# Half of the mask transposes of visits 6 to 21 moved from TensorE to VectorE in a masked graph attention kernel

## The chip, the cores and the metric

The kernel runs on one core of a Trainium2 chip. The metric is the device time of one execution in microseconds (us). An engine's name in the profile is PE for TensorE (matmuls; PEld is its weight load), DVE for VectorE, ACT for ScalarE, POOL for GpSimd and SP for SyncE, which here issues most of the loads.

## The reference, cut to what matters

```python
# x: (8192, 256) f32, adj: (8192, 8192) int32 of 0 and 1, a: (512, 1)
h = jnp.maximum(_layernorm(x, axis=-1), 0.0)
h1 = h @ a[:256];  h2 = h @ a[256:]
e = leaky_relu(h1 + h2.T, 0.01)
attention = jnp.where(adj > 0, e, -9e15)
attention = softmax(attention, axis=1)
out = x + attention @ h
```

The kernel uses that exp(leaky_relu(h1 + h2)) is, up to factors of row and column, a maximum of two terms. For a pair (i, j) it computes a weight W = max(r_i, g_j) times the mask bit, and sums W times (q_j h_j) over j. The row's own factor falls out in the division by the sum of weights.

## The kernel before, in words

**Tiles.** The 8192 rows and 8192 columns of adj are cut in blocks of 512. A *chunk* is one block of rows against one block of columns: 1 MB of int32, 256 chunks in all. A *visit* works one block of rows against 4 chunks (visits 0 to 24, 26, 28, ...) or 8 chunks (the odd visits from 25 on). `n` counts pairs of chunks; the chunk in a pair is `kc`, 0 (even) or 1 (odd), and a visit of 4 chunks has two values of n. A chunk has two *steps*, each of two tiles of 128 columns, so n has four steps k = 0 to 3, and `g` = 4n + k counts steps.

**One chunk goes through five engines.**

1. SP loads it to `adj_in[:, kc]` (`load_adj`), as soon as ACT has converted the chunk that stood there before, two chunks earlier. In visits 0 to 21 that is one DMA of 1 MB in rows of 2 KB (L271). From visit 22 on it is four DMAs of 256 KB whose pieces are 512 B long and lie turned in blocks of 32 (L268).
2. ACT makes a mask of 1-byte numbers, `mask8[:, kc]` (`convert`, L542).
3. The mask must stand with columns on the partitions. In visits 0 to 21 TensorE transposes it, four 128x128 tiles a chunk, into the PSUM tile `T[:, kc]` (L917). From visit 22 on (`N_MID` = 44 is the first n of that part, `dt` = `LATE` = 4) VectorE does it, with one transpose of 32x32 blocks (L767) over data loaded turned.
4. For each step DVE computes the weights (`weights`, L786, two instructions of 512 columns, from `T[:, kc]`), ACT rounds them to `w_hi` (`round_w`, L555 or L552), and DVE subtracts, which gives the rest `w_lo` (`subtract`, L801 or L797).
5. TensorE multiplies and sums into `acc`, 24 matmuls a step (`products`, L950, L952, L953), 48 a chunk.

**The order on each engine is written out by hand.** DVE's step k of n is: subtract of the step two before (g - 2), then side work if any, then the weights of g. `weights` waits until that subtraction is finished (`s_lo`), since it writes the buffer `W[:, k % 2]` that the subtraction read. `subtract` waits for ACT (`s_hi`), and for TensorE to have used the `w_lo` buffer of two steps before (`s_used`). TensorE in n does the products of step 0, transposes the even chunk of n + 1, does steps 1 and 2, transposes the odd chunk of n + 1, does step 3. ACT's order is convert of chunk (n, 1), rounding of steps 0 and 1, convert of chunk (n + 1, 0), rounding of steps 2 and 3, with side work after a rounding.

**Side work.** Visits 1 to 4 each prepare four further row tiles of h ("whole"). From visit 5 to 20 a pair of visits does it: visits 5, 7, ..., 19 ("early") the statistics (L728, four, then four aggregates L734), visits 6, 8, ..., 20 ("late") the scores (L754, eight instructions, two in each of steps 4 to 7 of the visit). ACT has the rows of h (L479, two at each of the last two steps of an early visit), exponentials (L493 to L497) at the end of a late one, and rounds h (L513) at the start of the next early one. At the start of each visit ACT empties `acc` to `stage` (L574), POOL adds the earlier partial sums from visit 9 on (L410), and a store and a load of 516 KB go to and from HBM.

Of the kernel before, what the change touches and what calls it, by code (L numbers as in the profile page):

```python
# [9 lines left out]
def masked_graph_attention(nc, x, adj, a, out):  # L10
# [35 lines left out]
    MID, LATE = 0, 4  # L46
    N_MID = 2 * 22

# [12 lines left out]
    with ctx:  # L61
# [126 lines left out]
        def run(eng, steps, h_made=None, h_summed=None):  # L188
# [13 lines left out]
            def quarter(v, q, prev, make=None, phase=None, made=None, nxt=None, head=False, turn=False,  # L202
                        dt=MID, dt_next=MID, deep=False):
# [16 lines left out]
            def two(j, q1, q2, prev1, prev2, nxt=None, dt=MID):  # L220
# [27 lines left out]
        def _(sp):  # L248
# [41 lines left out]
            def steps(V, n, c, first, second, last, third=False):  # L290
                if V.head and first:
                    load_x(0, 0, False)
                    sp.dma_start(r_rep[:, 1, :], a_row.partition_broadcast(P)).then_inc(s_a, 16)
                for kc in range(CI):
                    if V.head and not first:
                        load_x(c + kc, kc, True)
                    if V.head and first and kc == 1:
                        load_x(1, 1, False)
                        sp.dma_start(x_ahead, x_w[2]).then_inc(s_xa, 16)
                    load_adj(V.b, c + kc, n, kc, not (V.head and first), V.dt)  # L300
# [157 lines left out]
        def _(act):  # L458
# [72 lines left out]
            def convert(n, kc, wait, dt):  # L531

                if dt < G:
                    act.wait_ge(s_adj[kc], 16 * (n + 1))
                if dt:
                    act.wait_ge(s_turn[kc], 64 * (n - N_MID + 1))
                if dt == G and not (isinstance(n, int) and n == N_MID):
                    act.wait_ge(s_TV, (n - N_MID) * CI + kc - 1)
                elif wait:
                    act.wait_ge(s_T, n * CI + kc - 1)  # L540
# [72 lines left out]
            def begin():  # L613
# [5 lines left out]
                convert(0, 0, False, 0)  # L619
# [6 lines left out]
            def head_chunk(m):  # L626
# [7 lines left out]
                convert((m + 1) // CI, (m + 1) % CI, m > 0, 0)  # L634
# [80 lines left out]
        def _(dve):  # L715
# [53 lines left out]
            def weights(V, c, c_tot, g, k, wait, enter=False):

                if V.dt < G:
                    dve.wait_ge(s_T, c_tot + 1)
                if V.dt:
                    dve.wait_ge(s_TV, c_tot - CI * N_MID + 1)
# [78 lines left out]
            def steps(V, n, c, first, second, last, third=False):  # L853
# [3 lines left out]
                for k in range(PI):  # L857
                    kc = k // 2
                    g = n * PI + k
                    if V.head:  # L860
                        m = c + kc if V.head else None
                        dve.wait_ge(s_ex, m + 1)
                        weights(V, m, n * CI + kc, g, k, not (first and k < 2))
# [5 lines left out]
                    else:  # L869
                        if V.dt and k % 2 == 0:  # L870
# [7 lines left out]
                        weights(V, c + kc, n * CI + kc, g, k, True, enter)  # L878
# [26 lines left out]
        def _(pe):  # L905
# [78 lines left out]
            def steps(V, n, c, first, second, last, third=False):  # L984
# [6 lines left out]
                for k in range(PI):  # L991
# [15 lines left out]
                    if k % 2 == 0 and not V.head and not (V.tail and last):  # L1007
                        transpose_mask(n + 1, kc, True, V.dt_next if last else V.dt)
# [28 lines left out]
```

## Time and profile before

| | |
|---|---|
| time, 3 runs | median 1552.14 us (1547.85 to 1553.05) |
| the profiled execution | 1552.08 us, of which its span is 1550.3 us |
| PE busy | 1522.7 us, 98% of the span |
| PEld busy | 1511.9 us, 98% |
| DVE busy | 1489.6 us, 96% |
| ACT busy | 1162.5 us, 75% |
| POOL busy | 457.4 us, 30% |
| DMA | 331.05 MB, mean 214 GB/s |
| granted TensorE clock | 0.999 |

The span is from the first to the last instruction of the profiled execution; its own time is 1.8 us longer. Busy times of different engines lie beside each other. PE's busy time is no measure of how full it is, since matmuls overlap; how fast chunks follow one another is. Visits 6 to 21 lie between about 180 and 574 us of the span, and the seven pairs of visits 7 to 20 between about 205 and 549 us.

### The profile page before, as it was taken

To read this page: it belongs to the slowest core of one execution; us is meant where nothing else is said; L and a number is where in the kernel's file an instruction comes from. 1 tells how busy PE (TensorE), PEld (TensorE's weight loads), DVE (VectorE), ACT (ScalarE), POOL (GpSimd) and SP (SyncE) were. 2 spreads that over 40 slices of the span, in tenths; PEclk is the share of its full clock that TensorE was granted. 3 is DMA by queue.
4 is the path that set the end of the run, shared out by engine and by line. 5 is a ranking of instruction groups with operands and counts; after the bars stand their busy time and mean duration, and the time that the engine had idled before them with its cause. 6 is when DMAs were issued, how large, how long until landed. Compare 5 with 4: busy or idle time off the path is not lost.

```text
span 1550.3 us, 38852 instructions
## 1 busy us (share of the span) xinstructions
PE 1522.7 (98%) x12678; PEld 1511.9 (98%) x12678; DVE 1489.6 (96%) x2172; ACT 1162.5 (75%) x1180; POOL 457.4 (30%) x547
## 2 busy tenths in 40 slices
PE   5999999999999999999999999999999999999999
PEld 5999999999999999999999999999999999999998
DVE  7999999999999999999999999999999999999998
ACT  7787877778777777677776876777777777677774
POOL 6363334335452340120420320320320320420420
PEclk9999999999999999999999999999999999999999
DMA  6666677787778799999999999999999999999994
GB/s 211 222 200 230 206 223 227 230 248 221 245 220 254 220 225 233 221 201 206 218 207 207 224 204 207 226 197 210 230 195 205 228 195 207 217 195 209 219 199 98
DMA packets 436493, 331.05 MB, mean 214 GB/s; under 512 B 16704, under 2 KB 378176, under 8 KB 436416
## 3 DMA queue, kind: packets, MB, share of 16 engines
q1 hardware_dynamic: 411360, 288.94, 83.6%
q10 hardware_dynamic: 25056, 41.13, 8.7%
q8 instruction: 43, 0.70, 0.2%
q14 instruction: 34, 0.28, 0.1%
HBM read 308.90 MB, written 21.10 MB: 213 GB/s over the span
## 4 chain that ended last, share of the span: by engine, by line
PE 82%; DMA 5%; DVE 3%; ACT 3%; issue 2%; SPq 1%; ACTq 0%; DVEq 0%
PE acc L950 27%; PE acc L953 26%; PE acc L952 26%; DMA adj_in<-in_adj_dram 5%; PE T L917 2%; ACT mask L542 2%; DVE w_lo L797 1%; DVE halves L786 1%; SPq L268 1%; ACT w_hi L552 0%; DVE T L767 0%; DVE w_lo L801 0%; ACT w_hi L555 0%; DVE adj_in L901 0%; DVE adj_in L896 0%
## 5 line engine op out<-in xcount | busy, mean ns | idle before, releaser
L950 PE MATMUL acc<-h_hi,w_hi 128*128 128x258 f32 (+1 forms) x4096 | 1167.3, 285 | 9.2 <-DVE w_lo L801 3.4
L953 PE MATMUL acc<-h_hi,w_lo 128*128 128x258 f32 (+1 forms) x4096 | 1153.3, 282 | 0.0
L952 PE MATMUL acc<-h_lo,w_hi 128*128 128x256 f32 (+1 forms) x4096 | 1149.7, 281 | 0.0
L950 PEld LDWEIGHTS acc<-h_hi,w_hi 128*128 128x128 f32 x4096 | 771.8, 188 | 17.8 <-issue 8.0
L952 PEld LDWEIGHTS acc<-h_lo,w_hi 128*128 128x128 f32 x4096 | 778.4, 190 | 0.1
L953 PEld LDWEIGHTS acc<-h_hi,w_lo 128*128 128x128 f32 x4096 | 775.3, 189 | 0.0
L786 DVE SCALAR_TENSOR_TENSOR halves<-r_rep,g_all,T 128x512 f32<-128x512 f32 (+1 forms) x1024 | 712.7, 736 | 10.8 <-PE T L917 1.5
L542 ACT ACTIVATE mask<-adj_in,mhalf 128x2048 fp8e5<-128x2048 int32 x256 | 510.3, 1993 | 58.8 <-DMA adj_in<-in_adj_dram 58.5
L552 ACT ACTIVATE w_hi<-halves 128x1024 fp32r<-128x1024 f32 x336 | 353.6, 1057 | 185.0 <-DVE halves L786 172.3
L797 DVE SCALAR_TENSOR_TENSOR w_lo<-halves,w_hi 128x1024 fp32r<-128x1024 f32 x336 | 418.2, 1245 | 9.9 <-PE acc L953 4.9
L555 ACT ACTIVATE w_hi<-halves 128x1024 fp32r<-128x1024 f32 x176 | 185.3, 1057 | 97.5 <-DVE halves L786 92.6
L801 DVE SCALAR_TENSOR_TENSOR w_lo<-halves,w_hi 128x1024 fp32r<-128x1024 f32 x176 | 230.7, 1311 | 17.7 <-PE acc L953 9.1
L419 POOL TENSOR_TENSOR xb<-xb,stage 128x256 f32<-128x256 f32 x60 | 49.9, 831 | 584.7 <-ACT stage L606 584.3
L410 POOL TENSOR_TENSOR stage<-stage,xo 128x258 f32<-128x258 f32 x96 | 94.1, 1014 | 196.1 <-ACT stage L574 139.5
L767 DVE STREAM_TRANSPOSE T<-mask 128x512 f32<-128x512 f32 x168 | 120.6, 718 | 6.7 <-ACT mask L542 6.7
L382 POOL TENSOR_SCALAR halves<-halves,q 128x256 f32<-128x256 f32 x56 | 37.6, 690 | 201.5 <-ACT q L497 172.8
L574 ACT ACTIVATE stage<-acc 128x258 f32<-128x258 f32 x156 | 56.3, 383 | 25.4 <-PE acc L953 24.4
L426 POOL TENSOR_TENSOR xb<-xb,halves 128x256 f32<-128x256 f32 x60 | 69.0, 1151 | 9.1 <-POOL halves L423 7.4
L917 PE MATMUL T<-ident,mask 128*128 128x128 f32 x352 | 53.5, 274 | 14.6 <-ACT mask L542 14.6
L423 POOL TENSOR_SCALAR halves<-halves,fin 128x256 f32<-128x256 f32 x60 | 56.2, 937 | 0.0
L917 PEld LDWEIGHTS T<-ident,mask 128*128 128x128 f32 x352 | 41.1, 141 | 15.5 <-issue 12.5
L390 POOL TENSOR_TENSOR hsum<-hsum,halves 128x256 f32<-128x256 f32 x48 | 50.6, 1054 | 2.8
(70 smaller groups left out, 343.8 us busy)
## 6 DMA issues: line engine op xcount, KB each, us to landing
adj_in<-in_adj_dram SPq DMA_DIRECT2D x672, 256.0 KB, 5.0
adj_in<-in_adj_dram SPq DMA_DIRECT2D x88, 1024.0 KB, 6.3
part_sums<-stage ACTq DMA_DIRECT2D x24, 516.0 KB, 5.6
xo<-part_sums ACTq DMA_DIRECT2D x24, 516.0 KB, 4.4
r_rep<-r_rows SPq DMA_DIRECT2D x39, 256.0 KB, 4.8
xb<-in_x_dram ACTq DMA_DIRECT2D x15, 512.0 KB, 5.9
out_dram<-xb ACTq DMA_DIRECT2D x15, 512.0 KB, 4.7
xb<-in_x_dram SPq DMA_DIRECT2D x14, 512.0 KB, 5.8
```

The costliest lines, as they stand in the source:

```text
L410: last = nc.gpsimd.tensor_tensor(stage[:, t, :], stage[:, t, :], prior[:, t, :], ALU.add)
L542: nc.scalar.activation(mask8[:, kc, :, :].rearrange("p t j -> p (t j)"), adj_in[:, kc, :, :].rearrange("p t j -> p (t j)"), ACT.Sign, bias ...
L552: nc.scalar.activation(w_hi[:, k % HL, :].rearrange("p (u j) -> p u j", u=2), deep_w[k], ACT.Relu).then_inc(s_hi, 1)
L555: nc.scalar.activation(w_hi[:, k % HL, :], W[:, k % 2, :], ACT.Relu).then_inc(s_hi, 1)
L767: nc.vector.transpose(T[:, kc, t * P:], mask_words[:, kc, t:G, :]).then_inc(s_TV, 1)
L786: last = nc.vector.scalar_tensor_tensor(out, r_rep[:, V.v % 2, :], g_all[:, ds(G * c + e, 1)], T8[:, k // 2, e, :], ALU.max, ALU.mult)
L797: nc.vector.scalar_tensor_tensor(w_lo[:, k % LL, :].rearrange("p (u j) -> p u j", u=2), deep_w[k], 0.0, w_hi[:, k % HL, :].bitcast(f32).re ...
L801: nc.vector.scalar_tensor_tensor(w_lo[:, k % LL, :], W[:, k % 2, :], 0.0, w_hi[:, k % HL, :].bitcast(f32), ALU.max, ALU.subtract).then_inc ...
L917: last = nc.tensor.transpose(T[:, kc, t * P:(t + 1) * P], mask_words[:, kc, t, :], ident[:])
L950: nc.tensor.matmul(acc[:, t, 0:WC], w_hi[:, k % HL, cols], rhs_hi, start=start and u == 0, stop=False)
L952: nc.tensor.matmul(acc[:, t, 0:D], w_hi[:, k % HL, cols], rhs_lo, start=False, stop=False)
L953: last = nc.tensor.matmul(acc[:, t, 0:WC], w_lo[:, k % LL, cols], rhs_hi, start=False, stop=stop and u == 1)
```

## The change

In visits 6 to 21 (n = 12 to 43, 64 chunks) the even chunk of each n is handled as before: a plain load, four transposes by TensorE. The odd chunk is now loaded turned, with four DMAs, and transposed by one VectorE instruction. `dt` becomes a pair, one entry for each kc: `PLAIN` (0, 0), `ALT` (0, 4), `LATE` (4, 4). Visits 0 to 5 and 22 on stay as they were.

```diff
-    MID, LATE = 0, 4
+    PLAIN, ALT, LATE = (0, 0), (0, 4), (4, 4)
+    N_ALT = 2 * 6
     N_MID = 2 * 22
+    FIRST_TURNED = (N_MID, N_ALT)
+    def count_turned_by_tensor(n, kc, form):
+        return n * CI + kc + 1 if form == PLAIN else n + N_ALT + 1
+    def count_turned_by_vector(n, kc, form):
+        return n - N_ALT + 1 if form == ALT else N_MID - N_ALT + (n - N_MID) * CI + kc + 1
...
                 for q in range(4 if dt else 0):
-                    sp.dma_start(adj_in[32 * q:32 * q + 32, kc, G - dt:G, :],
-                                 adj_turned[b, :, 4 * (G - dt):4 * G, ds(c * BLK + q * P, P)]).then_inc(s_turn[kc], 16)
-                if dt < G:
-                    sp.dma_start(adj_in[:, kc, 0:G - dt, :], adj_v[b, :, 0:G - dt, ds(c * BLK, BLK)]
-                                 ).then_inc(s_adj[kc], 16)
+                    sp.dma_start(adj_in[32 * q:32 * q + 32, kc, :, :],
+                                 adj_turned[b, :, :, ds(c * BLK + q * P, P)]).then_inc(s_turn[kc], 16)
+                if not dt:
+                    sp.dma_start(adj_in[:, kc, :, :], adj_v[b, :, :, ds(c * BLK, BLK)]).then_inc(s_adj[kc], 16)
...
             def transpose_mask(V, n, kc):
-                if V.dt < G:
-                    dve.wait_ge(s_T, g + 1)
-                else:
-                    dve.wait_ge(s_mask, g + 1)
+                dve.wait_ge(s_mask, n * CI + kc + 1)
                 dve.sem_inc(s_vgate, 1)
-                nc.vector.transpose(T[:, kc, t * P:], mask_words[:, kc, t:G, :]).then_inc(s_TV, 1)
+                nc.vector.transpose(T[:, kc, :], mask_words[:, kc, :, :]).then_inc(s_TV, 1)
...
-                        if V.dt and k % 2 == 0:
+                        if V.dt == LATE and k % 2 == 0:
                             transpose_mask(V, n, kc)
...
-                        weights(V, c + kc, n * CI + kc, g, k, True, enter)
+                        if V.dt == ALT and k == 1:
+                            transpose_mask(V, n, 1)
+                        weights(V, c + kc, n, g, k, True, enter)
...
-                        transpose_mask(n + 1, kc, True, V.dt_next if last else V.dt)
+                        transpose_mask(n + 1, kc, True, (V.dt_next if last else V.dt)[kc])
```

`convert` waits in the same way as before, for the load and for whoever transposed the chunk that stood in `mask8[:, kc]`; `weights` waits for VectorE's count of transposes (`s_TV`) for an odd chunk of visits 6 to 21 and for TensorE's (`s_T`) for an even one.

On VectorE, at the start of visit 7, these rows stood before (L801 is a subtraction, L728 a statistic, L786 the two weights):

```order
L801 SCALAR_TENSOR_TENSOR w_lo<-halves,w_hi 128x1024
L786 SCALAR_TENSOR_TENSOR halves<-r_rep,g_all,T 128x512 x2
L801 SCALAR_TENSOR_TENSOR w_lo<-halves,w_hi 128x1024
L728 BN_STATS bst<-xb 128x6
L786 SCALAR_TENSOR_TENSOR halves<-r_rep,g_all,T 128x512 x2
L801 SCALAR_TENSOR_TENSOR w_lo<-halves,w_hi 128x1024
L728 BN_STATS bst<-xb 128x6
```

With the change the same place reads (L810 is the subtraction, L742 the statistic, L795 the weights, L776 the new transpose):

```order
L810 SCALAR_TENSOR_TENSOR w_lo<-halves,w_hi 128x1024
L795 SCALAR_TENSOR_TENSOR halves<-r_rep,g_all,T 128x512 x2
L810 SCALAR_TENSOR_TENSOR w_lo<-halves,w_hi 128x1024
L742 BN_STATS bst<-xb 128x6
L776 STREAM_TRANSPOSE T<-mask 128x512
L795 SCALAR_TENSOR_TENSOR halves<-r_rep,g_all,T 128x512 x2
L810 SCALAR_TENSOR_TENSOR w_lo<-halves,w_hi 128x1024
L742 BN_STATS bst<-xb 128x6
```

The transpose of chunk (n, 1) stands in step 1 of n, behind the side work and ahead of the weights of the even chunk, which do not need it. It needs ACT's convert of chunk (n, 1).

On SP, over visit 7 and the start of visit 8, these rows stood before (L271 is the plain load of a chunk, L261 the load of rows of x, L287 that of `r_rep`):

```order
L261 DMA xb<-in_x_dram 128x1024
L271 DMA adj_in<-in_adj_dram 128x4x512 x2
L287 DMA r_rep<-r_rows 128x512
L271 DMA adj_in<-in_adj_dram 128x4x512 x4
```

With the change there stands (L280 is the plain load, L277 the turned one, L270 the load of x, L295 that of `r_rep`):

```order
L270 DMA xb<-in_x_dram 128x1024
L277 DMA adj_in<-in_adj_dram 32x16x128 x4
L280 DMA adj_in<-in_adj_dram 128x4x512
L295 DMA r_rep<-r_rows 128x512
L277 DMA adj_in<-in_adj_dram 32x16x128 x4
L280 DMA adj_in<-in_adj_dram 128x4x512
L277 DMA adj_in<-in_adj_dram 32x16x128 x4
L280 DMA adj_in<-in_adj_dram 128x4x512
```

Each odd chunk is now four issues in place of one; the number of bytes is the same.

## Rows read from the trace of the kernel before

**Rows 1.** Windows: us, busy of PE, PEld, DVE, ACT, POOL, clock, DMA share, GB/s

```profile
204.60:549.00 344.40, 344.40 (x2915) 344.40 (x2913) 324.59 (x504) 269.13 (x307) 140.11 (x168) 1.00 0.75 232
574.30:597.40 23.10, 23.10 (x195) 23.05 (x194) 22.91 (x29) 17.07 (x17) 3.02 (x4) 1.00 1.14 229
1104.80:1196.00 91.20, 91.20 (x768) 91.07 (x767) 90.34 (x117) 66.90 (x57) 15.16 (x16) 1.00 1.04 210
```

**Rows 2.** The chain that ended last: start us, us, what; visits 1 to 20

```profile
97.58 0.44 PE T L917 x4
...
149.12 0.44 PE T L917 x4
...
204.61 0.44 PE T L917 x4
...
549.01 0.44 PE T L917 x4
```

**Rows 3.** VectorE's groups from 204.6 to 549.0 us: busy, mean ns | idle before

```profile
L801 DVE SCALAR_TENSOR_TENSOR w_lo<-halves,w_hi 128x1024 fp32r<-128x1024 f32 x112 | 148.1, 1323 | 12.7 <-PE acc L953 7.7 <-ACT w_hi L555 4.7
```

**Rows 4.** Timeline of VectorE, end of visit 13, start of visit 14

```profile
369.41 1.41 DVE L786 SCALAR_TENSOR_TENSOR halves<-r_rep,g_all,T 128x512 f32<-128x512 f32 x2
370.73 1.22 DVE L801 SCALAR_TENSOR_TENSOR w_lo<-halves,w_hi 128x1024 fp32r<-128x1024 f32 x1
372.05 1.41 DVE L786 SCALAR_TENSOR_TENSOR halves<-r_rep,g_all,T 128x512 f32<-128x512 f32 x2
373.99 1.23 DVE L801 SCALAR_TENSOR_TENSOR w_lo<-halves,w_hi 128x1024 fp32r<-128x1024 f32 x1 [0.53 <-PE acc L953]
```

**Rows 5.** Timeline of VectorE, a statistic and the aggregates (visit 11)

```profile
303.85 1.21 DVE L801 SCALAR_TENSOR_TENSOR w_lo<-halves,w_hi 128x1024 fp32r<-128x1024 f32 x1
304.98 0.41 DVE L728 BATCH_NORM_STATS2 bst<-xb 128x6 f32<-128x256 f32 x1
305.32 1.38 DVE L786 SCALAR_TENSOR_TENSOR halves<-r_rep,g_all,T 128x512 f32<-128x512 f32 x2
...
309.70 1.24 DVE L801 SCALAR_TENSOR_TENSOR w_lo<-halves,w_hi 128x1024 fp32r<-128x1024 f32 x1 [0.22 <-ACT w_hi L555]
...
311.73 0.72 DVE L786 SCALAR_TENSOR_TENSOR halves<-r_rep,g_all,T 128x512 f32<-128x512 f32 x1
```

**Rows 6.** Timeline of VectorE, a step with two scores (visit 2)

```profile
89.99 1.22 DVE L801 SCALAR_TENSOR_TENSOR w_lo<-halves,w_hi 128x1024 fp32r<-128x1024 f32 x1
...
91.80 1.40 DVE L786 SCALAR_TENSOR_TENSOR halves<-r_rep,g_all,T 128x512 f32<-128x512 int8 x2
```

**Rows 7.** Timeline of VectorE, a transpose of the late stretch

```profile
1304.37 0.72 DVE L767 STREAM_TRANSPOSE T<-mask 128x512 f32<-128x512 f32 x1
1305.00 1.20 DVE L797 SCALAR_TENSOR_TENSOR w_lo<-halves,w_hi 128x1024 fp32r<-128x1024 f32 x1
```

**Rows 8.** Timeline of ScalarE beside rows 4

```profile
370.85 1.06 ACT L555 ACTIVATE w_hi<-halves 128x1024 fp32r<-128x1024 f32 x1 [0.52 <-DVE halves L786]
371.81 1.08 ACT L479 ACTIVATE halves<-xb,shift,rstd 128x256 f32<-128x256 f32 x2
372.80 1.99 ACT L542 ACTIVATE mask<-adj_in,mhalf 128x2048 fp8e5<-128x2048 int32 x1
```

**Rows 9.** Plain load, line L271, from 204.6 to 549.0 us

```profile
L271 SPq DMA_DIRECT2D adj_in<-in_adj_dram x56: 367/372/383, 210.3 to 547.9; - x56
...
DMA to landing us min/median/max: 5.1/6.3/9.4
```

**Rows 10.** Turned load, line L268, from 574 to 621 us (visits 22, 23)

```profile
L268 SPq DMA_DIRECT2D adj_in<-in_adj_dram x32: 311/489/1721, 578.4 to 620.8; - x32
...
DMA to landing us min/median/max: 4.1/5.7/9.1
```

**Rows 11.** Waits from 545 to 640 us: us in total, times, longest

```profile
ACT mask L542 <- DMA adj_in<-in_adj_dram: 14.6, 9, 3.4
...
DVE T L767 <- ACT mask L542: 1.6, 2, 0.8
```

More of the change, by code:

```diff
@@ L218, in finals, with two @@
                             head=False, tail=tail, dt=LATE, dt_next=LATE, deep=True, rest=None))
-            def two(j, q1, q2, prev1, prev2, nxt=None, dt=MID):
+            def two(j, q1, q2, prev1, prev2, nxt=None, dt=ALT):
                 quarter(5 + 2 * j, q1, prev1, make=SH + j, phase="early", made=SH - 1 + j, nxt=nxt, dt=dt)
                 quarter(6 + 2 * j, q2, prev2, make=SH + j, phase="late", turn=q2 != q1)
-            quarter(0, 0, None, head=True, dt=0, dt_next=0)
-            quarter(1, 0, "first", make=Q, phase="whole", dt=0, dt_next=0)
+            quarter(0, 0, None, head=True, dt=PLAIN, dt_next=PLAIN)
+            quarter(1, 0, "first", make=Q, phase="whole", dt=PLAIN, dt_next=PLAIN)
             with eng.Fori(2, 5) as v:
-                quarter(v, 0, "first", make=v + 3, phase="whole", made=v + 2, dt=0, dt_next=0)
-            two(0, 0, 0, "first", "first", dt=0)
+                quarter(v, 0, "first", make=v + 3, phase="whole", made=v + 2, dt=PLAIN, dt_next=PLAIN)
+            two(0, 0, 0, "first", "first", dt=PLAIN)
             two(1, 0, 1, "first", "first", nxt=0)
@@ L299, in steps @@
                         sp.dma_start(x_ahead, x_w[2]).then_inc(s_xa, 16)
-                    load_adj(V.b, c + kc, n, kc, not (V.head and first), V.dt)
+                    load_adj(V.b, c + kc, n, kc, not (V.head and first), V.dt[kc])
                     if V.phase in ("early", "whole") and first and kc == 0:
@@ L529, in early_round_h, with convert @@
                                          scale=q4[:, parity, e:e + 1]).then_inc(s_hh if e == G - 1 else s_h0, 1)
-            def convert(n, kc, wait, dt):
-                if dt < G:
+            def convert(n, kc, wait, form):
+                if form[kc]:
+                    act.wait_ge(s_turn[kc], 64 * (n - FIRST_TURNED[kc] + 1))
+                else:
                     act.wait_ge(s_adj[kc], 16 * (n + 1))
[L535 to L538, printed above, removed]
+                was = form
+                if isinstance(n, int) and n == N_ALT and form == ALT:
+                    was = PLAIN
+                if isinstance(n, int) and n == N_MID:
+                    was = ALT
+                if wait and was[kc]:
+                    act.wait_ge(s_TV, count_turned_by_vector(n - 1, kc, was))
                 elif wait:
-                    act.wait_ge(s_T, n * CI + kc - 1)
+                    act.wait_ge(s_T, count_turned_by_tensor(n - 1, kc, was))
                 act.sem_inc(s_gate, 1)
@@ L618, in begin @@
                 h_rows(0, 0, range(G))
-                convert(0, 0, False, 0)
+                convert(0, 0, False, PLAIN)
                 exps(0, 0)
@@ L633, in head_chunk @@
                     h_rows(m + 1, (m + 1) % CI, [2, 3])
-                convert((m + 1) // CI, (m + 1) % CI, m > 0, 0)
+                convert((m + 1) // CI, (m + 1) % CI, m > 0, PLAIN)
                 round_w(2 * m + 1, (2 * m + 1) % PI, 2 * m + 1 >= HL)
@@ L758, in transpose_mask, with weights @@
             def transpose_mask(V, n, kc):
-                g = n * CI + kc
-                t = G - V.dt
-                if V.dt < G:
-                    dve.wait_ge(s_T, g + 1)
-                else:
-                    dve.wait_ge(s_mask, g + 1)
-                dve.sem_inc(s_vgate, 1)
-                nc.vector.transpose(T[:, kc, t * P:], mask_words[:, kc, t:G, :]).then_inc(s_TV, 1)
[L769 to L774, printed above, removed]
+                dve.wait_ge(s_mask, n * CI + kc + 1)
+                dve.sem_inc(s_vgate, 1)
+                nc.vector.transpose(T[:, kc, :], mask_words[:, kc, :, :]).then_inc(s_TV, 1)
+            def weights(V, c, n, g, k, wait, enter=False):
+                if V.dt[k // 2]:
+                    dve.wait_ge(s_TV, count_turned_by_vector(n, k // 2, V.dt))
+                else:
+                    dve.wait_ge(s_T, count_turned_by_tensor(n, k // 2, V.dt))
                 if wait and (not V.deep or enter):
@@ L862, in steps @@
                         dve.wait_ge(s_ex, m + 1)
-                        weights(V, m, n * CI + kc, g, k, not (first and k < 2))
+                        weights(V, m, n, g, k, not (first and k < 2))
                         if m + 1 < Q:
```

2 lines of the change are left out of this document (1 added, 1 removed).

## The prediction

> **What bounds the kernel now.** The busy times come first: PE is busy 98% of the span and DVE 96%, so two engines are candidates, and a share of busy time can't say which of them sets the pace. The chain that ended last decides it. In visits 7 to 20 it stays on PE; the transposes of L917 lie in it, 0.44 us for each four, and they recur twice for each n, that is once for each chunk: from 204.61 to 549.01 us are 344.4 us, 56 chunks, 6.15 us each [rows 2]. The window of the same stretch shows PE and PEld busy for all of it at a granted clock of 1.00 [rows 1]. So PE sets the pace there. In the late stretch, where it transposes nothing, PE gets through 768 matmuls, 16 chunks, in 91.2 us, 5.70 us each [rows 1]; 6.15 less 0.44 is 5.71, so 0.44 us is what a chunk's transposes cost on PE, and nothing else differs.
>
> The next thing to read is how much room DVE has in those visits. Its group of subtractions shows 12.7 us of idle time ahead of it, 7.7 for PE and 4.7 for ACT [rows 3]. That is 3.7% of the stretch. The change takes 3.6% of PE's work in a pair of chunks away and gives DVE an instruction, so it has to be seen whether DVE can follow.
>
> **DVE's work, step by step, from start to start.** A bare step is 1.32 us from weights to subtraction and 1.32 us from subtraction to weights: 369.41, 370.73, 372.05 [rows 4], 2.64 in all. With a statistic between subtraction and weights, it is 303.85 to 305.32, 1.47 us in place of 1.32: 0.15 more. The statistic itself takes 0.34, but it starts 1.13 us behind the subtraction, 0.19 earlier than the weights could, which wait for the subtraction's end [rows 5]. The fourth statistic with its aggregates makes it 2.03 us, 0.71 more [rows 5]. Two scores make it 1.81, 0.49 more [rows 6]. A pair of visits (16 steps) thus wants 16 x 2.64 + 3 x 0.15 + 0.71 + 4 x 0.49 = 45.4 us, the seven pairs of visits 7 to 20 want 317.5 us. Subtractions that run beside POOL's work are longer: the mean is 1.323 us against 1.22 bare [rows 3, 4], 112 x 0.10 = 11.3 us. Sum 328.8 us, the low bound of DVE's need. The high bound comes from the other side: 344.4 less the 12.4 us waited for PE and ACT is 332.0 [rows 1, 3]. A recorded wait is a little short (0.53 stands beside a start 1.94 us behind the weights where 1.32 was possible, 0.62 lost [rows 4]), so I take 330, nearer to the low bound.
>
> **What the change removes.** 32 odd chunks no longer pass through PE: 32 x 0.44 = 14.1 us off PE. In visits 7 to 20 PE then wants 344.4 - 28 x 0.44 = 332.1 us.
>
> **What it adds on DVE.** The transpose took 0.63 us from its start to the next instruction's start [rows 7]. Put between a subtraction and weights, it fills the 0.19 us of waiting there: 1.13 + 0.63 - 1.32 = 0.44 us net. In step 1 of an early visit's first n a statistic has already filled that gap, in step 1 of a late visit's second n two scores have; there it costs 0.63. A pair of visits has two of each kind: 2.14 us, seven pairs 15.0 us. The Trainium skill ("VectorE: DVE Perf Modes", section "The DRAIN you can't avoid") says that each VectorE instruction drains before the next whatever is waited for, and that a semaphore between two costs nothing extra. The trace disagrees by the 0.19 us of rows 4 and 5; by the rule all 32 transposes cost 0.63 us, 20.2 us in place of my 16.9, and the forecast would be 3.3 us higher.
>
> **A wait it adds.** The transpose in step 1 of n waits for ACT's convert of chunk (n, 1), and everything behind it on DVE waits with it, though the weights of step 1 need only the even chunk. PE waits for those in turn. At the start of a late visit ACT rounds the last step of the visit before, makes two rows of h, then converts: 370.85, 371.81, 372.80 to 374.79 us [rows 8]. DVE, had it not waited 0.62 us for PE there, would have been at the transpose at 372.05 + 1.32 + 1.13 = 374.50 [rows 4, 5]. So the transpose is 0.29 us late, in 7 of these visits: 2.0 us, and once more in visit 6. At other n ACT has exponentials (shorter), or DVE has side work in step 0 of the second n; there the convert is done first, but at the start of an early visit by some 0.2 us only.
>
> **The sum.** DVE's need in visits 7 to 20: 330 + 15.0 + 2.0 = 347.0 us, with the bounds 345.8 and 349.0, against 344.4 now and 332.1 that PE wants. DVE becomes the engine that sets the pace, all along: PE's steps would be 5.93 us a chunk in the mean, and DVE's 6.2. The stretch gains nothing and loses 2.6 us (1.4 to 4.6). Visit 6 is a late visit: its transposes cost DVE 0.44 + 0.63 + 0.29, with much the same room as the others, so about nothing. Visit 21 has no side work on DVE: 8 x 2.64 + 2 x 0.44 + about 1 for POOL = 23.0 us, so PE's 0.44 us of the one odd transpose that it had there are gained: -0.4.
>
> **The loads.** SP issues four DMAs for an odd chunk in place of one: 0.49 us each in the median where there was 0.37 [rows 9, 10], so the last is out 1.5 us later. For each GB/s the turned loads keep the DMA engines busier: 1.04 at 210 GB/s against 0.75 at 232 [rows 1]. Half the chunks turned, I estimate 0.75 + 85 x (1.04/210 - 0.75/232) = 0.90, under the 1.04 at which the late visits lose nothing. The slowest plain load took 9.4 us, and the slowest turned piece 9.1 [rows 9, 10]; an odd buffer is free for two chunks less a convert, 12.3 - 2.0 = 10.3 us. Slowest piece plus issue, 10.6, is just too long; the median, 5.7 + 1.5, has room. I put 1 us for it. It is hidden by ACT's own work elsewhere. The whole is +2.6 - 0.4 + 1 = +3.2 us on the profiled 1552.08 us, which lies at the median (1552.14): **1555 us**.
>
> **Rivals.**
>
> *A: DVE follows, PE keeps the pace.* All 14.1 us come back, 1538 us. For it: PE is full all the time and DVE idle 3.7%. Against it: DVE's need must be below 332.1 - 17.0 = 315 us in visits 7 to 20, and its bare instructions alone are 317.5. Visits 1 to 4 speak against it too: each has the side work of a whole pair, and its chunks follow at (149.12 - 97.58) / 8 = 6.44 us, 25.8 us a visit [rows 2]. There DVE already sets the pace, and my prices give 8 x 2.64 + 3.1 = 24.2 and some 0.6 for POOL, so they are short there, not long. I give it 0.05. A part of it is more likely: my prices of DVE are 2% too high (the subtractions beside POOL fall otherwise, or 330 hides waits), then -7 us, 1545. 0.09.
>
> *B: the forecast*, DVE's need within -4 and +4 us of the above: 0.56, own range 1551 to 1560.
>
> *C: the masks of odd chunks are late (the slower side).* In visits 22 and 23, with all chunks turned and the same partial sums stored and loaded, ACT waited for loads 9 times, 14.6 us in all over some 16 chunks [rows 11], where in visits 7 to 20 the same view lists no such wait. There the transposes lost only 1.6 us, but they stand at the start of step 2; in the changed visits they stand at step 1, about 1.5 us sooner. It decides once an odd load is more than ACT's 0.2 us of room late. The 13 visits 9 to 21 have such traffic, two odd chunks each; 26 x (14.6 / 16) = 24 us of late converts at most, less the room at each second n, about half: +10 us behind B, 1565 us. Half of the bytes being plain speaks against it. 0.30. The Trainium skill ("DMA: Bandwidth & Descriptors", section "Specifications") puts the smallest transfer for line rate at 512 B, which is just what a turned piece has. By it the share would stay at 0.75 and this rival would hardly be possible; the shares of rows 1 say that such pieces do cost more, so I keep it.
>
> **How the numbers follow.** What this kernel's measurement can tell from no change is 0.3%, 4.7 us. Faster by more: A and nearly all of its part, 0.13. Slower by more, above 1556.8: C's 0.30 and the upper part of B, 0.12: 0.42. Within: 0.45. The range runs from 1547, below which only A and a part of the second case lie (0.10), to 1566, above which a tenth lies.
>
> **What would show it.** In the windows of visits 7 to 20, PE's gaps appear and DVE's idle ahead of the subtractions (now 12.7 us) falls to nearly nothing; chunks follow at 6.15 to 6.25 us. The transposes have 0.72 us each and are followed at 0.63. DVE's waits list the transpose behind ACT's convert, 8 times for about 0.3 us; many more, or over 1 us, with ACT waiting for loads, is C. The DMA share rises to 0.90. If instead the chunks follow at 5.9 us with PE full, it is A, and my sum of DVE's need was wrong. The stretches before 180 and behind 574 us keep their length.

## The result, and the profile after

The changed kernel took 1555.97 us in the median of 11 runs (1551.56 to 1559.69), the kernel before 1552.29 beside it (1547.85 to 1555.48). The ratio is 1.0023, with a 95% interval of 1.0012 to 1.0034: slower by 3.7 us, less than the 0.3% named in the prediction. The profiled execution was the slowest of the 11 (1559.69 us, span 1557.8 against 1550.3 before). Of these 7.5 us, 2.8 lie behind visit 21 and 1.2 ahead of visit 1, where the program is the same; so the stretches are compared one by one.

The windows of the changed kernel over the first and the third stretch of [rows 1], with the same columns:

```profile
204.60:549.00 344.40, 335.86 (x2774) 331.07 (x2773) 335.92 (x529) 263.38 (x304) 134.62 (x165) 1.00 0.90 229
...
1104.80:1196.00 91.20, 90.44 (x754) 89.65 (x753) 89.13 (x115) 66.87 (x57) 18.14 (x20) 1.00 1.04 206
```

PE is no longer busy all the time in visits 7 to 20: 335.9 of 344.4 us, and PEld 331.1, at the same granted clock. DVE went from 324.6 to 335.9. The DMA share rose from 0.75 to 0.90 at nearly the same GB/s.

VectorE's groups of the changed kernel in the same stretch, busy time and mean ns, then idle time before them and what ended it:

```profile
L810 DVE SCALAR_TENSOR_TENSOR w_lo<-halves,w_hi 128x1024 fp32r<-128x1024 f32 x111 | 147.3, 1327 | 0.0
...
L776 DVE STREAM_TRANSPOSE T<-mask 128x512 f32<-128x512 f32 x28 | 20.1, 717 | 2.5 <-ACT mask L556 2.4
```

The 12.7 us that DVE waited ahead of its subtractions [rows 3] are gone, and 2.4 us of waits for the mask are new. The waits of PE, DVE and ACT in that stretch (us in all, times, longest) say who waits now:

```profile
PE acc L961 <- ACT w_hi L569: 3.3, 7, 0.6
PE acc L961 <- ACT stage L588: 3.3, 7, 0.5
DVE T L776 <- ACT mask L556: 2.4, 7, 0.3
...
ACT mask L556 <- DMA adj_in<-in_adj_dram: 0.9, 2, 0.5
```

PE waits for rounded weights and for emptied sums. Both hang on DVE's pace: ScalarE empties the sums behind a rounding, and at 379.23 us that rounding had waited 1.32 us for DVE's weights. Loads are late for 0.9 us only. VectorE's timeline at the start of visit 14 is the place of [rows 4]:

```profile
372.91 1.22 DVE L810 SCALAR_TENSOR_TENSOR w_lo<-halves,w_hi 128x1024 fp32r<-128x1024 f32 x1
374.23 1.41 DVE L795 SCALAR_TENSOR_TENSOR halves<-r_rep,g_all,T 128x512 f32<-128x512 f32 x2
375.56 1.22 DVE L810 SCALAR_TENSOR_TENSOR w_lo<-halves,w_hi 128x1024 fp32r<-128x1024 f32 x1
377.12 0.73 DVE L776 STREAM_TRANSPOSE T<-mask 128x512 f32<-128x512 f32 x1 [0.35 <-ACT mask L556]
377.75 1.36 DVE L795 SCALAR_TENSOR_TENSOR halves<-r_rep,g_all,T 128x512 f32<-128x512 f32 x2
379.04 1.22 DVE L810 SCALAR_TENSOR_TENSOR w_lo<-halves,w_hi 128x1024 fp32r<-128x1024 f32 x1
380.36 1.41 DVE L795 SCALAR_TENSOR_TENSOR halves<-r_rep,g_all,T 128x512 f32<-128x512 f32 x2
381.68 1.76 DVE L810 SCALAR_TENSOR_TENSOR w_lo<-halves,w_hi 128x1024 fp32r<-128x1024 f32 x1
```

The subtraction at 375.56 follows the weights after 1.33 us, where it waited for PE before. The transpose then waits 0.35 us for the mask, and the next instruction follows 0.63 us behind it.

From here on the *stretch* is measured on VectorE, from the first weights of visit 7 to the first of visit 21. The two rows of the changed kernel are

```profile
201.75 1.41 DVE L795 SCALAR_TENSOR_TENSOR halves<-r_rep,g_all,T 128x512 f32<-128x512 f32 x2
...
549.60 1.41 DVE L795 SCALAR_TENSOR_TENSOR halves<-r_rep,g_all,T 128x512 f32<-128x512 f32 x2
```

so 347.8 us. In the kernel before they are

```profile
200.48 0.75 DVE L786 SCALAR_TENSOR_TENSOR halves<-r_rep,g_all,T 128x512 f32<-128x512 f32 x1
...
545.50 0.75 DVE L786 SCALAR_TENSOR_TENSOR halves<-r_rep,g_all,T 128x512 f32<-128x512 f32 x1
```

so 345.0 us. The change costs 2.8 us there. By the same measure visit 6 took 0.2 us less and visit 21 0.7 us more.

Taken pair by pair, the change does not cost the same everywhere. Visits 7 and 8 took 48.2 us where they had taken 49.2: a gain of 1.0 us. The six later pairs took 49.91 to 49.96 us each, where five had taken 49.2 and one 49.8. POOL adds earlier partial sums only from visit 9 on; the subtractions of visits 7 and 8 are lengthened by 0.2 us in all, those of the later pairs by 1.3 to 2.1 us a pair.

Each length comes from one trace of each kernel, so it matters how much such a length varies from one trace to the next. Visits 1 to 5 are the same program in eleven of the fourteen traces, and took 124.8 to 125.2 us in each. The part behind visit 21 varied by 5.5 us over the same eleven (978.3 to 983.8). So the stretch tells the experiments apart better than their total times do.

### The profile page after: what moved, and what is told of

It reads as the page before. It is cut to its first block, busy times and chain, and to the rows that moved or that the text cites. A ratio compares the mean times of both kernels' runs of the same rounds, so it can differ in the third digit from the quotient of the medians.

```text
span 1557.8 us, 38905 instructions
## 1 busy us (share of the span) xinstructions
PE 1518.2 (97%) x12550; PEld 1501.7 (96%) x12550; DVE 1506.6 (97%) x2204; ACT 1160.2 (74%) x1180; POOL 454.8 (29%) x547
## 4 chain that ended last, share of the span: by engine, by line
PE 52%; DVE 16%; DMA 10%; issue 9%; ACT 6%; SPq 2%; DVEq 1%; POOL 0%; ACTq 0%
PE acc L961 18%; PE acc L964 17%; PE acc L963 17%; DMA adj_in<-in_adj_dram 10%; DVE halves L795 6%; DVE w_lo L810 6%; ACT mask L556 4%; DVE w_lo L806 2%; SPq L277 2%; ACT w_hi L566 1%; PE T L928 1%; DVE T L776 1%; DVE xo L768 1%; DMA xo<-part_sums 0%; ACT halves L487 0%
## 5 line engine op out<-in xcount | busy, mean ns | idle before, releaser
L961 PE MATMUL acc<-h_hi,w_hi 128*128 128x258 f32 (+1 forms) x4096 | 1169.0, 285 | 21.1 <-DVE w_lo L806 6.4
L961 PEld LDWEIGHTS acc<-h_hi,w_hi 128*128 128x128 f32 x4096 | 772.1, 189 | 35.6 <-issue 12.7
L795 DVE SCALAR_TENSOR_TENSOR halves<-r_rep,g_all,T 128x512 f32<-128x512 f32 (+1 forms) x1024 | 710.9, 733 | 10.0 <-PE T L928 2.6
L806 DVE SCALAR_TENSOR_TENSOR w_lo<-halves,w_hi 128x1024 fp32r<-128x1024 f32 x336 | 418.3, 1245 | 10.4 <-PE acc L964 5.0
L810 DVE SCALAR_TENSOR_TENSOR w_lo<-halves,w_hi 128x1024 fp32r<-128x1024 f32 x176 | 232.2, 1319 | 3.4 <-ACT w_hi L569 3.2
L427 POOL TENSOR_TENSOR xb<-xb,stage 128x256 f32<-128x256 f32 x60 | 56.6, 943 | 586.7 <-ACT stage L620 522.7
L776 DVE STREAM_TRANSPOSE T<-mask 128x512 f32<-128x512 f32 x200 | 143.5, 718 | 11.0 <-ACT mask L556 10.9
L588 ACT ACTIVATE stage<-acc 128x258 f32<-128x258 f32 x156 | 52.5, 381 | 13.6 <-PE acc L964 12.5
L928 PE MATMUL T<-ident,mask 128*128 128x128 f32 x224 | 34.5, 277 | 14.7 <-ACT mask L556 14.7
L431 POOL TENSOR_SCALAR halves<-halves,fin 128x256 f32<-128x256 f32 x60 | 48.0, 800 | 0.0
L407 POOL TENSOR_TENSOR h_lo<-halves,h_hi 128x256 f32 (+1 forms) x48 | 46.7, 1001 | 3.5 <-ACT h_hi L524 3.5
L398 POOL TENSOR_TENSOR hsum<-hsum,halves 128x256 f32<-128x256 f32 x48 | 46.0, 958 | 2.8
```

Of the source, the lines that this page charges most:

```text
L776: nc.vector.transpose(T[:, kc, :], mask_words[:, kc, :, :]).then_inc(s_TV, 1)
L795: last = nc.vector.scalar_tensor_tensor(out, r_rep[:, V.v % 2, :], g_all[:, ds(G * c + e, 1)], T8[:, k // 2, e, :], ALU.max, ALU.mult)
L806: nc.vector.scalar_tensor_tensor(w_lo[:, k % LL, :].rearrange("p (u j) -> p u j", u=2), deep_w[k], 0.0, w_hi[:, k % HL, :].bitcast(f32).re ...
L810: nc.vector.scalar_tensor_tensor(w_lo[:, k % LL, :], W[:, k % 2, :], 0.0, w_hi[:, k % HL, :].bitcast(f32), ALU.max, ALU.subtract).then_inc ...
L961: nc.tensor.matmul(acc[:, t, 0:WC], w_hi[:, k % HL, cols], rhs_hi, start=start and u == 0, stop=False)
```

## The experiments

Each ratio is to the kernel before, run on the same chip in between; the stretch is from the run's profile.

**Theory 1, as predicted:** VectorE's need, summed over its instructions, is the length of the stretch, and TensorE's relief is time that nobody can use. **Rival:** late loads and masks of odd chunks. The edits below are against the changed kernel unless said otherwise.

### e1: TensorE's part alone, nearly

```diff
-                nc.vector.transpose(T[:, kc, :], mask_words[:, kc, :, :]).then_inc(s_TV, 1)
+                if V.dt == ALT:
+                    nc.vector.transpose(T[:, kc, 0:P], mask_words[:, kc, 0:1, :]).then_inc(s_TV, 1)
...
```

> The changed kernel, but VectorE's 32 new transposes handle 32 columns of the 512 (a quarter of one tile), so masks of odd chunks of visits 6 to 21 are wrong; waits, loads and TensorE's share stay. My theory (VectorE's need sets the pace): its need in visits 7 to 20 falls from 347 us by nearly the whole 15 us of the transposes to some 333, about TensorE's own 332, so 1541 to 1546 us, 6 to 11 below the kernel before. Rival (late masks or dearer loads of odd chunks set the pace): they are unchanged, so the time stays at 1553 to 1557.

Measured: 1550.26 us, ratio 0.9997 (0.9985 to 1.0008), stretch 343.3 us. Neither theory's number. The edit leaves 128 of the 512 columns, not the 32 that the expectation speaks of. The stretch lost 4.5 us of the 15 expected. The groups and the short transpose in the timeline show why:

```profile
L813 DVE SCALAR_TENSOR_TENSOR w_lo<-halves,w_hi 128x1024 fp32r<-128x1024 f32 x113 | 152.7, 1351 | 3.3 <-ACT w_hi L569 3.3
...
L777 DVE STREAM_TRANSPOSE T<-mask 128x128 f32<-128x128 f32 x28 | 8.9, 317 | 2.5 <-ACT mask L556 2.5
...
311.77 0.32 DVE L777 STREAM_TRANSPOSE T<-mask 128x128 f32<-128x128 f32 x1
312.00 0.70 DVE L798 SCALAR_TENSOR_TENSOR halves<-r_rep,g_all,T 128x512 f32<-128x512 f32 x1
```

The short transpose still takes 0.23 us where the whole one takes 0.63, so only 28 x 0.40 = 11.2 us were taken off. DVE still waits 2.5 us for masks. And two things grew: 3.3 us of waits for ACT came back, and the mean subtraction went from 1.327 to 1.351 us, 2.7 us over 112.

### e2: TensorE's old work given back

```diff
+                if dt == G and kc == 1 and (not isinstance(n, int) or n < N_MID):
+                    for t in range(G):
+                        nc.tensor.transpose(hs_ps[:, 2 * P:3 * P], ident[:], ident[:])
...
```

> The changed kernel, and TensorE also makes four transposes of the identity into an unused corner of PSUM where it transposed the odd chunks before, so it has all of its old work. My theory: TensorE has that time to spare (it wants 332 us of 348), so the time stays that of the changed kernel, 1555 to 1558 us. Rival (both engines limit in turn, and TensorE's relief pays for a good part of VectorE's load): up to 32 x 0.44 = 14 us come on top, at least 5: 1561 to 1570.

Measured: 1557.81 us, ratio 1.0052 (1.0034 to 1.0070), stretch 349.7 us, 1.8 us more than the changed kernel's. TensorE has 28 x 0.44 = 12.3 us more to do and the stretch feels 1.8 of it. The first theory holds for most of it, the rival's 5 us at least do not appear; "worth nothing" is a little too strong. More than half of the 1.8 us lies in one place: visits 7 and 8 went back from 48.2 to 49.2 us, which is TensorE's old pace. There TensorE's relief did count. The six later pairs grew by 0.1 us each.

### e6 and e7: the same work off VectorE, after and before

```diff
-                        nc.vector.scalar_tensor_tensor(out[j], h[:, e, :], 1.0, a_ps[:, j * D:(j + 1) * D],
+                        nc.vector.scalar_tensor_tensor(out[j][:, 0:w], h[:, e, 0:w], 1.0, a_ps[:, j * D:j * D + w],
...
```

The width `w` is 16 for the scores of visits 6 to 20, else D.

> The changed kernel with the 64 scores of visits 6 to 20 cut from 256 to 16 columns (the scores are wrong): VectorE has 0.49 us less at each of 32 steps, 15.7 us. My theory: VectorE's need in visits 7 to 20 falls by 13.7 to about 333 us, TensorE's is 332, so 1541 to 1546 us. Rival (masks and loads of odd chunks are late): no change against the changed kernel, 1554 to 1557.

> The kernel before with the same cut of the scores. My theory: there TensorE sets the pace and VectorE has room, so the same 15.7 us off VectorE give nothing: 1551 to 1553 us. Rival (VectorE limited the kernel before as well, in the steps with side work): up to 5 us come back, 1547.

Measured, after: 1542.18 us, ratio 0.9955 (0.9938 to 0.9972), stretch 337.5 us, 10.4 less. Measured, before: 1552.14 us, ratio 1.0003 (0.9991 to 1.0015), stretch 344.4 us, 0.6 less. This is the plainest pair: what is taken off VectorE shows in the one kernel and not in the other. (The 13.7 us taken off in the stretch gave 10.4, and DVE's waits rose by 1.9.) In the kernel before it only becomes waiting, 22.8 us ahead of the subtractions where [rows 3] had 12.7:

```profile
L801 DVE SCALAR_TENSOR_TENSOR w_lo<-halves,w_hi 128x1024 fp32r<-128x1024 f32 x112 | 148.0, 1321 | 22.8 <-PE acc L953 15.4 <-ACT w_hi L555 5.9 <-issue 0.2
```

### e5: the loads alone

Against the changed kernel: VectorE's new transpose is left out, TensorE transposes every chunk up to visit 21 as before, and the odd chunks stay loaded turned (their masks are then of other elements).

> The kernel before with the odd chunks of visits 6 to 21 loaded turned, by four DMAs, but still transposed by TensorE, so their masks are wrong: the load's part of the change alone. My theory: the loads are hidden, 1552 to 1553 us, DMA share 0.90 in visits 7 to 20, at most 1 us of waits of ScalarE for loads. Rival (the dearer loads are part of the loss): 1554 to 1557.

Measured: 1552.35 us, ratio 1.0001 (0.9989 to 1.0013), stretch 345.1 us, against 345.0 of the kernel before, with ACT waiting 1.1 us for loads in all. Its window:

```profile
204.60:549.00 344.40, 344.40 (x2913) 344.35 (x2913) 326.21 (x503) 270.37 (x310) 139.21 (x167) 1.00 0.91 231
```

The DMA engines are busier, 0.91 for 0.75, and nobody is later. The loads are no part of the loss.

### e3 and e4: the wait for the mask

```diff
 e3: the transpose at step 2, ahead of the subtraction
-                        if V.dt == LATE and k % 2 == 0:
+                        if V.dt == LATE and k % 2 == 0 or V.dt == ALT and k == 2:
                             transpose_mask(V, n, kc)
...
-                        if V.dt == ALT and k == 1:
-                            transpose_mask(V, n, 1)
 e4: two rows of h moved from step 7 of an early visit to step 0 of the late one, on ScalarE
-                    if k == 7:
-                        h_rows(V.make, 0, [2, 3])
+                if V.phase == "late" and k == 0:
+                    h_rows(V.make, 0, [2, 3])
```

> The changed kernel with the transpose of an odd chunk one place later, ahead of the subtraction of step 2, as it stands in visits 22 on. My theory: it no longer fills the 0.19 us between a subtraction and the weights (17 of 32 places lose that), +3.2 us, but it doesn't wait for ACT's convert any more, -2.3: 1556 to 1558 us, and the waits of the transpose vanish. Rival (late masks cost more than their recorded 2.4 us): faster than the changed kernel by 3 or more, 1553 or less.

> The changed kernel with the last two rows of h of an early visit made by ScalarE behind its first convert and rounding of the late visit, not ahead of them. My theory: the eight waits of the transpose for the convert at the start of late visits (0.35 us each) vanish, -2.5 us: 1553 to 1554 us; some of it may come back, since the emptying of the sums is later. Rival (those waits are hidden by TensorE's idle time or cost nothing): no change, 1556.

Measured, e3: 1558.43 us, ratio 1.0038 (1.0022 to 1.0054), stretch 348.9 us. The waits for the mask are gone and it is still 1.1 us longer than the changed kernel's. That is near the expectation, but by other terms too. The scores now wait 4.8 us for POOL's additions (0.6 in the changed kernel) and the subtractions 2.1 us for ACT, and the mean subtraction fell from 1.327 to 1.267 us, 6.7 us over 112:

```profile
L810 DVE SCALAR_TENSOR_TENSOR w_lo<-halves,w_hi 128x1024 fp32r<-128x1024 f32 x110 | 139.3, 1267 | 2.1 <-ACT w_hi L569 2.1
L768 DVE SCALAR_TENSOR_TENSOR xo<-halves,a_ps 128x256 f32<-128x256 f32 x56 | 21.1, 413 | 4.8 <-POOL stage L418 4.8
```

Measured, e4: 1554.01 us, ratio 1.0013 (1.0003 to 1.0023), stretch 345.9 us, 1.9 us shorter. The waits of the transpose vanish from its view, and 3.6 us of waits of the subtraction for ACT appear. DVE's waits are thus no fewer (3.6 for 3.0 us), and what fell is the lengthening of the subtractions, by 2.0 us. Neither run isolates what the wait for the mask costs at the end of the stretch.

### e11: POOL's part

```diff
-                    nc.gpsimd.tensor_tensor(hsum[:], hsum[:], hb[:, e, :], ALU.add).then_inc(s_hs, 1)
+                    nc.gpsimd.tensor_tensor(hsum[:, 0:16], hsum[:, 0:16], hb[:, e, 0:16], ALU.add).then_inc(s_hs, 1)
...
-                    last = nc.gpsimd.tensor_tensor(stage[:, t, :], stage[:, t, :], prior[:, t, :], ALU.add)
+                    last = nc.gpsimd.tensor_tensor(stage[:, t, 0:16], stage[:, t, 0:16], prior[:, t, 0:16], ALU.add)
```

> The changed kernel with POOL's additions of earlier partial sums and of rows of h cut from 256 or 258 to 16 columns (the sums are wrong). Of the 12.1 us by which subtractions are lengthened in visits 7 to 20, 9.6 lie beside these. Theory (VectorE's need sets the pace, and POOL's share is in it): the stretch falls from 347.8 to 338 to 340 us, the time to 1546 to 1549. Rival (a lengthened subtraction costs nothing, since something else is late then): 346 or more, no change in the time.

Measured: 1541.51 us, ratio 0.9935 (0.9922 to 0.9949), stretch 338.6 us, 9.2 less. The subtraction's mean fell from 1.327 to 1.242 us, 112 x 0.085 = 9.5 us:

```profile
L810 DVE SCALAR_TENSOR_TENSOR w_lo<-halves,w_hi 128x1024 fp32r<-128x1024 f32 x114 | 141.6, 1242 | 0.3
```

In the changed kernel VectorE waits for POOL's additions only once in the stretch, 0.6 us. They slow it by lengthening its subtractions. All seven pairs of visits now took 48.1 to 48.8 us, less than the kernel before, as only the first had done. The time fell by more than was expected (1546 to 1549). POOL's additions stand in other visits too: visits 1 to 5 took 1.2 us less and visit 21 1.3 us less. The rest is not accounted for.

### e8 and e12: half as many transposes on VectorE

A version that should suit both engines: VectorE takes the odd chunk of one n of each visit only, 16 in all.

```diff
+    def by_vector(form, kc, second):
+        return form == LATE or form == ALT and kc == 1 and second
...
-                        if V.dt == ALT and k == 1:
+                        if V.dt == ALT and k == 1 and second:
...
```

This is e8. In e12 the two conditions read `not second` and `first`. In both, the counts that ACT and DVE wait for are changed to match.

> The changed kernel, but only the odd chunk of each visit's second n goes to VectorE (16 chunks), that of the first n stays with TensorE. My theory: a pair of visits then wants 49.2 - 0.88 = 48.3 us of TensorE and 47.1 + 0.44 + 0.63 = 48.2 of VectorE, and no transpose waits for a mask: 0.8 us less a pair than before, 5 to 7 in all: 1546 to 1549 us, faster than both kernels. Rival (either engine stalls the other whenever both are near full): most of it is lost, 1551 to 1554.

Measured, e8: 1555.23 us, ratio 1.0021 (1.0006 to 1.0037), stretch 346.4 us. My expectation failed: its time is no better than the changed kernel's (the stretch is 1.4 us shorter), though VectorE waited 8.6 us in the stretch and TensorE had only 344.4 - 14 x 0.44 = 338 us of work:

```profile
L820 DVE SCALAR_TENSOR_TENSOR w_lo<-halves,w_hi 128x1024 fp32r<-128x1024 f32 x112 | 147.6, 1318 | 8.6 <-ACT w_hi L580 3.9 <-PE acc L974 3.9
...
331.55 1.23 DVE L820 SCALAR_TENSOR_TENSOR w_lo<-halves,w_hi 128x1024 fp32r<-128x1024 f32 x1 [0.55 <-PE acc L974]
...
334.82 1.75 DVE L820 SCALAR_TENSOR_TENSOR w_lo<-halves,w_hi 128x1024 fp32r<-128x1024 f32 x1 [0.54 <-ACT w_hi L580]
```

These waits stand in steps 2 and 3 of a late visit; the scores and the transpose come in steps 4 to 7. **Theory 2:** room at the start of a late visit can't be carried to the steps with scores, since `w_lo` holds two steps and DVE can't go further ahead. The kernel before had the same pattern: of its waits ahead of subtractions, 12.6 us in the stretch, 11.2 lie in steps 0 to 3 of the late visits. In the other steps DVE hardly waited, so there it had no room for a transpose.

> Only the odd chunk of each visit's first n goes to VectorE (16 chunks), that of the second n stays with TensorE: the same numbers of transposes on either engine as in the run with second n only, at other places. Theory (the room lies at the start of a late visit): the transpose of the late visit falls into it and costs nothing; that of the early visit stands among the statistics, 0.63 us. Visits 7 to 20 take 342 to 344 us, where the other placing took 346.4. Rival (only the number of transposes counts): 346 us.

Measured, e12: 1549.95 us, ratio 0.9996 (0.9987 to 1.0005), stretch 344.6 us: the same numbers of transposes, 1.8 us less. The place counts, as theory 2 has it, though the gain is smaller than expected, and the stretch lies 0.6 us above the range given. That the two buffers of `w_lo` are the reason is argued from the program; no run has more of them. VectorE is full again:

```profile
L820 DVE SCALAR_TENSOR_TENSOR w_lo<-halves,w_hi 128x1024 fp32r<-128x1024 f32 x113 | 153.3, 1357 | 1.0 <-PE acc L974 0.6 <-ACT w_hi L580 0.4
...
L789 DVE STREAM_TRANSPOSE T<-mask 128x512 f32<-128x512 f32 x14 | 10.0, 715 | 2.1 <-ACT mask L567 2.1
```

The mean subtraction rose to 1.357 us. It is the fastest of the complete versions, and not to be told from the kernel before.

### e9 and e10: the scores at other steps

The scores of a late visit at steps 2, 3, 4 and 6, in e9 over e8, in e10 over the changed kernel. Their scratch output had to go to `xb`, so SP's load of x got a wait for the scores. The scores' own wait for POOL's additions fell away with the old output:

```diff
+                if not isinstance(c, int) or c > SH:
+                    sp.sem_inc(s_lgate, 1)
+                    sp.wait_ge(s_dot, 2 * G * c + 2)
                 sp.sem_inc(s_lgate, 1)
                 sp.dma_start(x_bufs[0], x_w[c]).then_inc(s_x[0], 16)
...
-                if V.phase == "late" and k >= 4:
-                    if k == 4 and V.prev == "added":
-                        dve.wait_ge(s_add, V.pa + 1)
-                    scores(V.make, 0, [k - 4])
+                if V.phase == "late" and k in (2, 3, 4, 6):
+                    scores(V.make, 0, [(2, 3, 4, 6).index(k)], spread=True)
```

> The kernel with only the odd chunk of each visit's second n on VectorE, and the scores of a late visit at its steps 2, 3, 4 and 6 in place of 4 to 7. In the run without this move VectorE waited 10 us ahead of its subtractions in visits 7 to 20, and yet TensorE had gaps of 1.5 us a pair of visits. New theory: VectorE's room lies at the start of a late visit and can't be carried to the steps with scores, since w_lo holds only two steps; with scores put into that room the stretch of visits 7 to 20 falls from 346.4 to about 342 us. Rival (the gaps come from ScalarE's order or POOL, not from where the room lies): 345 us or more.

> The changed kernel with the same move of the scores. Both theories have VectorE without any wait for TensorE there, so its sum alone counts: the stretch of visits 7 to 20 stays at 347 to 348.5 us. If it falls by over 2 us, then where the scores stand matters even when VectorE is full, and the sum over its instructions is not what sets the pace.

Measured, e9: 1571.44 us, ratio 1.0125 (1.0110 to 1.0141), stretch 348.1 us. Measured, e10: 1594.78 us, ratio 1.0273 (1.0259 to 1.0287), stretch 371.2 us. Both are spoiled by the wait that I added, and tell nothing on theory 2. Visits 1 to 5, whose scores did not move, took 139.9 us in e9 and 143.4 in e10, where 125.1 had been enough. In e10 the wait held SP's queue 7 times, 60.8 us, and the loads of adj stand behind it:

```profile
SPq L272 <- DVE xb L773: 60.8, 7, 9.1
...
ACT mask L559 <- DMA adj_in<-in_adj_dram: 29.4, 8, 5.3
DVE T L781 <- ACT mask L559: 25.9, 7, 4.7
```

e10 gives an idea of what rival C would have been: masks late by up to 4.7 us, 25.9 us in 7 waits, and 23.4 us on the stretch. The granted clock was down as well, 0.95 in the stretch and 0.67 in the 10 us from 330 us on, so how much of the 23.4 us is the late masks' is not separated.

## Why the prediction was right, point by point

**DVE's sum sets the pace.** e6 against e7 shows it, and e2 from TensorE's side. With the prices of the prediction and each run's own groups, the stretch can also be put together: 317.5 us of bare steps and side work, the transposes net, the mean subtraction's excess over 1.22 us times 112, and the recorded waits of DVE.

| run | transposes | lengthening | waits | sum | stretch |
|---|---|---|---|---|---|
| before | 0 | 11.5 | 12.7 | 341.7 | 345.0 |
| changed | 15.0 | 12.0 | 3.0 | 347.5 | 347.8 |
| e1 | 3.8 | 14.7 | 6.4 | 342.4 | 343.3 |
| e2 | 15.0 | 9.4 | 7.1 | 349.0 | 349.7 |
| e3 | 17.6 | 5.3 | 6.9 | 347.3 | 348.9 |
| e4 | 15.0 | 10.0 | 3.6 | 346.1 | 345.9 |
| e5 | 0 | 13.2 | 11.1 | 341.8 | 345.1 |
| e6 (303.8 in place of 317.5) | 15.0 | 12.2 | 4.9 | 335.9 | 337.5 |
| e7 (303.8 in place of 317.5) | 0 | 11.3 | 22.8 | 337.9 | 344.4 |
| e8 | 7.5 | 11.0 | 8.6 | 344.6 | 346.4 |
| e11 | 15.0 | 2.5 | 3.3 | 338.3 | 338.6 |
| e12 | 7.5 | 15.3 | 3.7 | 344.0 | 344.6 |

(e1: 28 x 0.23 less 14 gaps of 0.19; e3: 28 x 0.63. Waits are those ahead of subtractions, transposes and scores.) In six runs the sum comes within 1 us. In five it is 1.6 to 3.3 us short, and in e7, where DVE waits most, 6.5. A recorded wait is short by 0.09 us (0.53 for 0.62 [rows 4]), which makes 2.6 us for the 29 waits of the kernel before and 4.4 for the 49 of e7; the rest is open. Since waits are a term of it, the sum comes out for the kernel before as well, where TensorE sets the pace. It bears out the prices, not who sets the pace. The prediction gave 347.0 for the changed kernel, with bounds of 345.8 and 349.0.

**The transpose at 0.44 or 0.63 us.** The trace has 0.63 from its start to the next instruction's, and 15.0 us net fit the sum. The 0.19 us that it fills behind a subtraction is real, and can be read in the changed kernel:

```profile
364.40 1.21 DVE L810 SCALAR_TENSOR_TENSOR w_lo<-halves,w_hi 128x1024 fp32r<-128x1024 f32 x1
365.54 0.71 DVE L776 STREAM_TRANSPOSE T<-mask 128x512 f32<-128x512 f32 x1
366.17 0.70 DVE L795 SCALAR_TENSOR_TENSOR halves<-r_rep,g_all,T 128x512 f32<-128x512 f32 x1
```

From subtraction to weights are 1.77 us in place of 1.32, so the transpose costs 0.45. In e3 it stands between weights and subtraction, where it fills nothing:

```profile
366.31 1.40 DVE L795 SCALAR_TENSOR_TENSOR halves<-r_rep,g_all,T 128x512 f32<-128x512 f32 x2
367.63 0.72 DVE L776 STREAM_TRANSPOSE T<-mask 128x512 f32<-128x512 f32 x1
368.26 1.20 DVE L810 SCALAR_TENSOR_TENSOR w_lo<-halves,w_hi 128x1024 fp32r<-128x1024 f32 x1
```

That is 1.95 us in place of 1.32, and the whole 0.63. So the rule by which all 32 would cost 0.63 us, and the forecast 3.3 us more, does not hold here.

**The wait for the mask.** Forecast 0.29 us in 7 visits, 2.0 us; measured 2.4 us in 7 waits. That it holds up VectorE's next instructions is seen at 377.12 us. What it is worth at the end is not shown: e4 took it away and gained 1.9 us, but with as much waiting elsewhere.

**The loads.** The share went to 0.90, as estimated, and e5 shows no loss. The 1 us that I put on them was too much; ACT waited 0.9 us in the whole stretch and none of it can be seen in the time.

**Visit 21** was wrong in sign: I had it gain 0.4 us, it lost 0.7. I gave POOL 1 us there; the four subtractions at 554 to 564 us took 1.57, 1.77, 1.67 and 1.67 us, 1.8 us over bare in all, beside three groups of additions that POOL did without a pause from 553.0 to 565.6 us. And I left out a term. Visit 22's first transpose stands ahead of that visit's first weights, so it lies in this stretch and costs 0.63 us (572.12 us). With both, VectorE's need is 21.1 + 0.9 + 1.8 + 0.6 = 24.4 us, and 24.5 were measured, against 23.8 before. VectorE, not TensorE, sets the pace in visit 21 too.

**Luck in the total.** The forecast was +3.2 us. By the stretches it is +2.8 - 0.2 + 0.7 = +3.3, and the medians differ by 3.7. But visit 21 was 1.1 us worse than forecast and the loads 1.0 us better, and that these two cancel is luck. The +2.6 us of the stretch is a mean as well, of a gain in the first pair of visits and losses in the others, which the prediction, with POOL's share spread evenly, did not have.

**Two things the prediction took for fixed are not.** POOL's lengthening was a constant 11.3 us in it, and ranged from 5.3 to 15.3 us over e1 to e8 and e12, with the same work on POOL, as the two engines' instructions meet otherwise. And 330 us of need with 15 us of room was read as room for 15 us of work. e8 shows that room in the wrong steps buys nothing (its stretch is 1.4 us longer than before), and e12 that taking half the transposes off lets the lengthening grow by 3.3 us. This is why no share of this change between the engines was found that beats the kernel before. Whether the lengthening grew because DVE no longer waits, or by chance of the order, is open. What the scores at other steps would give, without a wait in SP's queue, is open too.

## What to carry to other kernels

Before work is moved to an engine that is 94% busy, sum its instructions from start to start, with the waits that they fill and the neighbours that stretch them, and set it against the pace that the kernel has now: here 330 + 15 + 2 = 347 against 344.4 us told the sign of the change, and TensorE's new need, 332 us, lay below both. Idle time of that engine counts as room only if it lies in the steps where the new work goes, or if buffers let it run ahead. And look where the neighbours' work is absent: the same change gained 1.0 us in the one pair of visits where POOL adds no partial sums.

## What the runs showed of the hardware

- A subtraction with two inputs in SBUF takes 1.22 us alone, and up to 1.8 beside POOL's additions; the weights, whose mask comes from PSUM, took 1.40 us for two in the midst of the same additions (383.55 us, in additions from 381.61 to 385.45), and 1.41 away from them. The lengthening by additions was worth 9.5 us of one stretch (e11). The Trainium skill says the same of the two kinds ("SBUF — State Buffer", section "Who interferes with whom"): VectorE with two SBUF inputs contends with a GpSimd instruction that reads SBUF, and with at most one, outside its 2-port modes, it doesn't. The trace agrees, with 0.35 to 0.55 us for each of the four subtractions at 554 to 564 us.
- With half of the chunks loaded in pieces of 512 B the DMA engines were at a share of 0.91 (e5), where pieces of 2 KB alone had 0.75, at the same GB/s (231, 232).
- A VectorE transpose of a quarter of the columns (128 for 512) still cost 0.23 us against 0.63 (e1).
- Where PE stood idle for long in e10 (24.7 us of waits for emptied sums in the stretch), the granted clock of the stretch was 0.95, that is, in part at the lower of its two levels (1.2 and 2.4 GHz). All other runs had 1.00 in that stretch.
